# Two chained transformer layers on one core: the order of the work within a beat rebuilt on all engines

## The reference

```python
n = _layer_norm(x, ln1_g, ln1_b)
x = x + _attention(n, n, a1_wq, a1_wk, a1_wv, a1_wo, a1_bo)
n = _layer_norm(x, ln2_g, ln2_b)
x = x + _attention(n, context, a2_wq, a2_wk, a2_wv, a2_wo, a2_bo)
x = _geglu_ff(_layer_norm(x, ln3_g, ln3_b), ff_w1, ff_b1, ff_w2, ff_b2) + x
...
probs_t = jax.nn.softmax(scores_t, axis=-1)
text_out = jnp.einsum('bhst,bhtd->bhsd', probs_t, v_t)
qsem = _l2norm(jnp.einsum('bhst,bte->bhse', probs_t, text_ehs))
sem = jnp.einsum('bhse,bne->bhsn', qsem, _l2norm(ip_ehs))
probs_ip = jax.nn.softmax(attn_scores + SEM_SCALE * sem, axis=-1) * spatial_mask[None, None, :, None]
out = (text_out + ip_out) @ W_out + b_out + residual
```

## Time and profile before

| | us |
|---|---|
| median of 2 runs (4306.78 and 4325.45) | 4316.11 |
| the profiled execution | 4322.96 |
| its span, first to last instruction | 4321.2 |
| mean granted TensorE clock in it | 0.935 of full |

### The profile page before, as it was taken

The page is one execution under the profiler, slowest core; times in us unless marked ns, Lnnn a source line. Parts: engine busy times, 40 slices in busy tenths (PEclk is TensorE's granted clock), DMA queues, the critical chain, the costliest instruction groups (busy, mean ns, idle before and its releaser), DMA issues.

```text
span 4321.2 us, 96000 instructions
## 1 busy us (share of the span) xinstructions
PE 3645.5 (84%) x34752; PEld 3346.6 (77%) x34752; DVE 2540.2 (59%) x7677; ACT 2432.8 (56%) x6547; POOL 1337.3 (31%) x1657
## 2 busy tenths in 40 slices
PE   6889888888888988889788898888889888897887
PEld 5778778787777878878787787877778787787876
DVE  6546565565656656565565555656566565655654
ACT  4465555555555565565555655555555655655553
POOL 2223332333333323333233323333333233332322
PEclk8999999999999999999999989999999999999985
DMA  5422212222221312213122121322213222131210
GB/s 157 138 60 85 73 50 89 56 86 68 61 88 50 98 57 74 84 46 94 52 88 71 50 89 54 91 66 61 88 49 95 58 73 84 43 98 51 81 41 9
DMA packets 210732, 313.83 MB, mean 73 GB/s; under 512 B 31232, under 2 KB 167520, under 8 KB 210272
## 3 DMA queue, kind: packets, MB, share of 16 engines
q1 hardware_dynamic: 209984, 307.53, 24.3%
q10 hardware_dynamic: 288, 0.16, 0.0%
HBM read 267.97 MB, written 14.42 MB: 65 GB/s over the span
## 4 chain that ended last, share of the span: by engine, by line
PE 56%; DVE 22%; ACT 12%; issue 10%; POOL 0%; DMA 0%; SPq 0%; DVEq 0%; ACTq 0%; POOLq 0%
PE PG L623 7%; PE PW L755 5%; PE PV L809 5%; PE PS L775 5%; PE PG L598 4%; PE PV L858 4%; ACT SE L977 4%; PE PG L615 4%; PE PT L793 4%; DVE mx L1231 3%; PE PG L599 2%; PE PG L601 2%; PE PG L600 2%; PE PT L841 2%; PE PG L699 2%
## 5 line engine op out<-in xcount | busy, mean ns | idle before, releaser
L1433 POOL TENSOR_TENSOR SE<-SE,rs 128x512 f32<-128x512 f32 (+1 forms) x640 | 558.8, 873 | 2016.0 <-DVE rs L1253 2016.0
L977 ACT ACTIVATE SE<-PS,mx 128x77 f32<-128x77 f32 (+1 forms) x2560 | 677.6, 360 | 141.6 <-DVE mx L1231 140.2
L1426 POOL TENSOR_TENSOR n<-qq,p_half 128x4 f32<-128x4 f32 x320 | 323.4, 1010 | 688.8 <-DVE qq L1276 688.8
L965 ACT ACTIVATE PTs<-PT 128x1024 f32<-128x1024 f32 (+1 forms) x320 | 327.0, 1022 | 365.1 <-PE PT L793 365.1
L1169 DVE COPY v_sb<-PG 128x512 f32<-128x512 f32 (+1 forms) x320 | 220.5, 689 | 376.2 <-PE PG L623 219.3
L1248 DVE TENSOR_REDUCE sums<-SE 128x4 f32<-128x512 f32 (+1 forms) x640 | 365.7, 571 | 120.8 <-ACT SE L977 119.3
L995 ACT ACTIVATE SE<-PT,mx 128x73 f32<-128x73 f32 x1280 | 304.5, 325 | 208.8 <-DVE mx L1240 157.8
L755 PE MATMUL PW<-w_o,OTs 128*128 128x160 f32 x2560 | 404.8, 301 | 0.0
L913 ACT ACTIVATE qk<-PG 128x512 f32<-128x512 f32 (+1 forms) x640 | 328.6, 513 | 116.1 <-PE PG L601 109.7
L809 PE MATMUL PV<-PTs,v_sb 128*64 128x128 f32 (+1 forms) x5120 | 392.9, 301 | 0.0
L793 PE MATMUL PT<-ident,SE 64*128 64x64 f32 (+1 forms) x5120 | 255.8, 244 | 160.1 <-issue 155.0
(11 more groups left out here) (207 smaller groups left out, 8800.4 us busy)
## 6 DMA issues: line engine op xcount, KB each, us to landing
q_slice<-q_split SPq DMA_DIRECT2D x630, 192.0 KB, 2.4
vc_slice<-vc_split SPq DMA_DIRECT2D x155, 512.0 KB, 3.7
kc_slice<-kc_split SPq DMA_DIRECT2D x150, 256.0 KB, 2.7
q1st<-q_hi SPq DMA_DIRECT2D x320, 32.0 KB, 1.8
k1st<-k_hi SPq DMA_DIRECT2D x160, 38.5 KB, 2.2
xres<-in_x_dram SPq DMA_DIRECT2D x32, 160.0 KB, 2.4
q1st<-q_lo SPq DMA_DIRECT2D x160, 32.0 KB, 1.9
out_dram<-x SPq DMA_DIRECT2D x64, 80.0 KB, 1.9
```

The costliest lines, as they stand in the source:

```text
L965: a_(PTs[0:J, q % 2, :, :].rearrange("p u (i r k) -> p r (u i) k", r=2, k=64), PT[0:J, :, :].rearrange("p r (x k) -> p r x k", k=64), ACT. ...
L977: last = a_(SE[:, n % 4, J * i:J * i + J], PS[:, e, J * at:J * at + J], ACT.Exp, bias=mx[:, q % 2, 4 * e + at:4 * e + at + 1])
L1433: gp.tensor_tensor(e, e, rs[:, n % 2, :].unsqueeze(2).to_broadcast([128, 4, J]), ALU.mult)\
```

## The change

Nothing is computed otherwise. What moves:

- **PE**: layer 1's `probs_transposed1` and `scores1` come first in slot 1, ahead of the second `qk` job; `probs_v1` comes first in slot 2, ahead of `wo`.
- **ACT**: `exp1` moves from slot 0 of the next beat to slot 2 of its own beat; `pt1_out` moves ahead of the second `exp`.
- **DVE**: `softmax1_in` moves from slot 2 to slot 1, between the two `prob_sums`; the `v` read-out goes behind the second `prob_sums`; the sum of squares leaves `unit_out` and becomes `unit_norms`, right behind the maximum of slot 0 one beat later; the norm's pieces and the context's scaling go right behind it, `norm_out` three slots after `norm_stats`; `unit_out` goes ahead of `block_out`.
- **POOL**: `norms_of` one beat later, in slot 0; `rstd_of` and `add_bias` in the slot of the statistics.
- **Slots**: norms, `ff`, `down`, `q1`, context, x and tail jobs get other slots (most late jobs now stand in slot 2), `L1_BEAT` becomes `BEATS + 2`; the tail of an image is spread over 12 slots, not 8.
- **Buffers**: the gated tile `gl` moves from `shared` into rows 0 and 1 of `kx`, the cross-attention keys, free at that time; `csq` moves into row 9 of `kx`. The context's loads no longer wait for `ff`.

```diff
-    NORM_SLOT = {(0, 0): -16, (0, 1): -1, (1, 0): 17, (1, 1): 32, (2, 0): 47, (2, 1): 62, (3, 0): 56, (3, 1): 71}
-    FF_SLOT = [51, 52, 53, 53, 54, 66, 67, 68, 68, 69]
+    NORM_SLOT = {(0, 0): 42, (0, 1): 3, (1, 0): 18, (1, 1): 33, (2, 0): 48, (2, 1): 69, (3, 0): 60, (3, 1): 84}
+    NEXT_GROUP = {(0, 0)}
+    TURN_AFTER = [5, 5, 4, 1]
+    FF_SLOT = [53, 53, 53, 56, 56, 74, 74, 74, 77, 77]
...
-    PREP_SLOT = [14, 20]
-    X_SLOT = [11, 57]
-    L1_BEAT = BEATS + 1
+    PREP_SLOT = [-5, 13]
+    CONTEXT_SLOT = [-12, 0]
+    X_SLOT = [24, 60]
+    L1_BEAT = BEATS + 2
...
+    TAIL_JOB = {"ipT": 7, "ip": 9, "oT1": 10, "y": 12}
...
-        cin, gl = shared[0:TS, :, :], shared[:, :, :]
+        cin = shared[0:TS, :, :]
...
+        gl = kx[:, 0:2, 0:HT]
...
-            + [(t + (1 if k == 3 else 3), ("xT", g, k, h)) for t, g, k, h in NORMS]
+            + [(t + TURN_AFTER[k], ("xT", g, k, h)) for t, g, k, h in NORMS]
...
-            + [(STEP * g + PREP_SLOT[h] + 3, ("cT", g, h)) for g in range(GROUPS) for h in range(2)]
-            + [(tail_slot(g, b) + d, (kind, g, b)) for d, kind in ((5, "ipT"), (6, "ip"), (7, "oT1"), (8, "y"))
+            + [(STEP * g + PREP_SLOT[h] + 4, ("cT", g, h)) for g in range(GROUPS) for h in range(2)]
+            + [(tail_slot(g, b) + d, (kind, g, b)) for kind, d in TAIL_JOB.items()
...
+                    if part == 1 and l1_at(beat - 1):
+                        probs_transposed1(*l1_at(beat - 1), turned)
+                    if part == 1 and l1_at(beat):
+                        scores1(*l1_at(beat), turned)
                     for name in qk_at(t):
                         job(name)
                     for name in late_at(t):
                         if name[0] == "v":
                             job(name)
-                    if part == 1 and l1_at(beat - 1):
-                        probs_transposed1(*l1_at(beat - 1), turned)
-                    if part == 1 and l1_at(beat):
-                        scores1(*l1_at(beat), turned)
+                    if part == 2 and l1_at(beat - 1):
+                        probs_v1(*l1_at(beat - 1), multiplied)
...
-                    if sub == 0 and l1_at(beat - 1):
-                        exp1(*l1_at(beat - 1))
                     if sub == 0 and duo_at(beat):
                         pt_out(*duo_at(beat))
+                    if sub == 1 and l1_at(beat - 1):
+                        pt1_out(*l1_at(beat - 1))
...
-                    if sub == 1 and l1_at(beat - 1):
-                        pt1_out(*l1_at(beat - 1))
+                    if sub == 2 and l1_at(beat):
+                        exp1(*l1_at(beat))
...
+                    if sub == 0 and l1_at(beat - 2):
+                        unit_norms(*l1_at(beat - 2))
                     for g, h in preps_at(t - 2):
                         context_scale(g, h)
...
-                    for g, k, h in norms_at(t - 2):
+                    for g, k, h in norms_at(t - 3):
                         if k < 3:
                             norm_out(g, k, h)
```

More of the change, by code:

```diff
@@ L355, in norm_slot @@
             own = FIRST_NORM_SLOT if g == 0 else {}
-            return STEP * g + own.get((k, h), NORM_SLOT[(k, h)])
+            return STEP * (g - ((k, h) in NEXT_GROUP)) + own.get((k, h), NORM_SLOT[(k, h)])
         NORMS = sorted((norm_slot(g, k, h), g, k, h) for g in range(GROUPS) for k, h in NORM_SLOT)
@@ L885, in _ @@
                         wo(g, 2 * d + 1)
-                    if part == 2 and l1_at(beat - 1):
-                        probs_v1(*l1_at(beat - 1), multiplied)
                     for name in late_at(t):
@@ L1003, in context_squares @@
                         act.wait_ge(S["c_dve"], HB * (2 * g + h))
-                    if g > 0:
-                        for w in range(W1):
-                            act.wait_ge(S[f"k1_in{w}"], 16 * 3 * g)
                     for b in range(HB):
@@ L1458, in _ @@
                         normalise(g, 2 * d + 1)
[L1459 removed]
+                    for g, k, h in norms_at(t):
                         if k < 3:
@@ L1469, in _ @@
                         gp.tensor_tensor(cst[:, 1, :], cst[:, 0, :], p_half[0:TS, 0:HB], ALU.pow).then_inc(S["c_pow"], 1)
-                    if sub == 2 and l1_at(beat - 1):
-                        norms_of(*l1_at(beat - 1))
+                    if sub == 0 and l1_at(beat - 2):
+                        norms_of(*l1_at(beat - 2))
 _INS = ['x', 'ctx_2048', 'fside_S_0',
```

78 lines of the change are left out of this document (39 added, 39 removed).

## The result

The changed kernel takes 3682.97 us (median of 2 runs, 3681.71 to 3684.23) against 4316.11 before: ratio 0.853, 95% interval 0.845 to 0.861. The forecast was 4005 with a range of 3880 to 4190, so the sign was right and the gain, 633 us, was twice the 312 of the sum.

The account below looks back on a forecast made before the run. PE's work order and waits bound the kernel: 36.8 us idle a group less 14.0 and 5.0 leaves 17.8, plus 3.0 clock, times 15 is 312; edges 0. From 4322.96 to 4011, median 4005 us, range 3880 to 4190.

Parts of the forecast that it names:

- What goes: PE's listed waits in a full group, such as L793 (155.0 us) and `nx` (116.5): all 36.8 us of idle time removed.
- What comes: New PE waits the new order brings to each full group, four items from a walk through the engines' lists: 14.0 us.
- Late jobs of slot 1: Jobs right behind `v` wait for the second `qk` bank in six self-attention beats: 3.6 us a group.
- The Exp table's return: ACT's table load behind `pt_out` in four beats delays both `exp` and `qk` read-outs: 2.8 us a group.
- Bank chains: Slot 2 waits on PE: feed-forward piece behind context transposes 2.1, `k1` behind `xT` 1.35, `vip` 1.1; together 4.5 us.
- the allowance: Idle time put back on PE for waits the hand-made list missed: 0.25 us a beat, 5.0 a group.
- the clock: PE's busy time returned by a higher granted clock as idle time falls: 3 us a group, bounds 0 and 10.
- the edges: Group 0 and the tail behind the last scores: 5 us back on one, +5 on the other, together 0.
- Bound by PE alone: Rival: allowance not needed and clock returns with idle time, 440 us gained, 3877 us; 13%.
- The loop of DVE and ACT: Rival: this loop sets self-attention beats, adding 1.1 us a beat over ten beats, 11 a group: 4170 us; 18%.
- Slower, ACT the engine waited for: Rival: `exp1` comes later than PE's next L793, a wait in every beat costing 400 us: 4405 us; 4%.
- Norm pieces beside POOL: `norm_out` on DVE beside POOL's power op, 0 to 1.0 us added to each: taken as 0, 90 us if uncovered.

Follow-up runs that it names:

- a mere filler: Four dummy matmuls put ahead of PE's wait for `exp1` (before `probs_transposed`) in the kernel before: 4305.7 us, ratio 0.999.
- the parts put back: Changed kernel with one part put back at a time: `exp1` 3938.9 us, feed-forward pieces spread 3908.4, norm pieces ahead of the maximum 3876.8, layer 1's maximum in slot 2 3882.9.
- the two edits on listed waits: Changed kernel with `pt1_out` behind the second `qk` read-out: 3675.0 us; changed kernel with late jobs reordered (`k1`, `vip` ahead of `xT`, `cT` last): 3687.9.
- the first experiment: Kernel before with only layer 1's `exp1` moved to slot 2 of its own beat: 4303.8 us, ratio 0.997.
- the fastest version: Changed kernel with `pt1_out` behind the second `qk` read-out in 13 beats of 20: 3602.1 us; with `cT` also last in its slot 3601.1.

## Why the forecast was half the gain

*What goes* was right, row by row, for the waits themselves: L793 155.0 to 3.7, `nx` 116.5 to 16.5, no releaser of the earlier trace rows left among the large ones. It was not right as a set of separate amounts, though the sum did not need that: the 155.0 of L793 alone are worth 14 us (with 60 table loads more), and the whole set 633.

*What comes, 14.0 a group*: group 7 has 13.4, the mean is 13.0. By items:

1. Late jobs of slot 1, 3.6. PE waits 0.68, 0.68, 0.67, 0.87, 1.24 and 0.68 in the six beats: 4.8. Of the 1.24, 0.56 belong to the next item. Two rows of group 7:

```profile
1622.31 0.39 PE L608 MATMUL PG<-w_v_hi,nT 128*128 128x256 f32 x1 [0.34 <-ACT qk L915]
1624.76 0.54 PE L733 MATMUL PG<-vbd_sb,ipTs 80*128 80x160 f32 x2 [1.24 <-ACT qk L915]
```

2. The Exp table's return, 2.8. `v` waits 0.34 to 0.37 in three of the four beats, as in the first of these rows, and the late job behind it the 0.56: 1.6.
3. Bank chains, 4.5. They are 1.47, 1.55 and 0.88: 3.9. The first two in group 7:

```profile
1614.50 0.39 PE L600 MATMUL PG<-nT,w_hi 128*128 128x256 f32 x1 [1.47 <-DVE cipT L1150]
```

```profile
1720.63 1.17 PE L617 MATMUL PG<-cT,w_k1h 128*128 128x328 f32 x6 [1.55 <-DVE nT L1157]
```

4. Key beats, 3.1. `v` waits 0.28 in four beats and 0.45 in one, and smaller ones follow: 2.9. One that was not listed, 0.75 before `probs_v` behind the end of `unit_out`, makes the rest.

**The first step that failed is the allowance**, 5.0 us a group "since a list made by hand misses waits". The walk had missed one wait of 0.75; the kernel has 24.7 us less idle time a group, the list said 22.8, the sum took 17.8. Of these 6.9, 5.0 are the allowance, 0.9 that the mean group had 37.7 us of idle time and group 7 had 36.8, and 1.0 that less came than was listed. Over 15 groups this is 103 us.

**The second is the clock**, 3 us a group, where busy time fell by 14.4. Two errors lie in it. The forecast kept the light matmuls as a reason for the low clock; but they are as many as before, and the clock came back (26.6 to 4.2 us a group), as it did with a mere filler. And the forecast knew of no other way in which busy time could shrink; the upper bound of 10 was too low for that. A wait also makes the first matmuls behind it slow. Rows of the changed kernel, a `qk` job in flow and `v` behind a wait, both at the full clock:

```profile
1607.76 0.28 PE L600 MATMUL PG<-nT,q_slice 128*128 128x256 f32 x1
1607.88 0.28 PE L601 MATMUL PG<-nT,q_slice 128*128 128x256 f32 x1
...
1609.24 0.39 PE L608 MATMUL PG<-w_v_hi,nT 128*128 128x256 f32 x1 [0.36 <-ACT qk L915]
1609.46 0.28 PE L609 MATMUL PG<-w_v_lo,nT 128*128 128x256 f32 x1
```

In flow the starts are 0.12 apart; behind the wait the first takes 0.22 to the second, 0.39 to its end, and the pipeline's end before it (0.28 behind the last start) counts as busy while nothing new begins. In the stretch of the earlier trace rows at the lower clock the same jobs start 0.21 apart. Over the 16 kernels of this study without fillers, the means per group (1 to 14) lie on a line: busy time = 204.5 + 0.51 x idle time, correlation 0.97; from 13.0 us idle and 209.4 busy (changed) over 19.5 and 215.7 (norms before the maximum) to 37.7 and 223.9 (before). How the 0.51 divides between clock and restarts the runs tell only roughly, since the two go together: with both in the fit a microsecond at the lower clock adds 0.36 of busy time and one of idle time 0.22. From 26.6 to 4.2 that is 8 us for the clock and from 37.7 to 13.0 5.4 for the restarts, near the 14.4.

The groups of one kernel part the two better, since they hold the same instructions in the same order and still differ in their clock. Two groups of the kernel before (PE's columns alone):

```profile
1285.96:1545.27 259.31, 219.07 (x2175) 0.97 0.25 72
2330.82:2600.11 269.29, 234.68 (x2175) 0.90 0.24 69
```

With the clock not rounded, the low-clock time is 13.7 and 51.2 us. Over groups 2 to 14 a microsecond of it adds 0.41 us of busy time in the kernel before (r = 1.00) and takes 0.15 of idle time away, so the group is 0.26 longer; in the changed kernel it adds 0.47 and idle time stays at 13.2 to 13.4. Without any low-clock time the lines end at 213.4 and 208.5 us of busy time. So of the 14.4 us some 9.5 are the clock and some 4.9 are there at the full clock too. Restarts would account for these: a group of before has 43 waits above 0.05 us on average, a changed one 24, and each costs by the rows above about 0.26 us of busy time (0.10 in the first start and 0.16 of the pipeline's end), so the 19 fewer are worth 4.9 us, an estimate. The same two groups have one order of instructions and two clocks, so the order alone does not set the clock. Nor does the amount of idle time alone: layer 1's chain alone in the kernel before took 7.6 us of idle time from a group, and its low-clock time did not fall.

Over 15 groups the step is short by 171 us.

**The third is the edges**, taken as nothing: 60 us. Group 0 lost 21 us of idle time and 11 of busy time. It has the same norm and context transposes as every group, whose waits I had counted for full groups only: in group 0's window of before PE waits 10.2 us for `nx` and 4.8 for `shared`, and the beats with them were 3 to 6 us longer than they are now. The tail lost 28 us, which went back when `exp1` was put back and partly (12 us) with layer 1's maximum: the steps of layer 1 there have nothing of layer 0 beside them, so the lateness of the chain stood in each. `exp1` alone in the kernel before took 2 us off the tail, the chain 12. It takes 6.2 us a step now (143.68 over 23) in place of 7.8. I had used the 7.8 for the step added and did not ask why it was 7.8.

103 + 171 + 60 is 334, where the forecast was 327 above the profiled execution (4011 against 3684). The 7 too many are group 15, counted here as a full group: it gained 32 us where the mean of the others is 39.

The rivals. *Bound by PE alone* (3877, 13%) was the right one in kind and still too small, by the clock's step and the edges. *The loop of DVE and ACT* did not add its 1.1 us a beat. That the engines' lists do bind is seen from the parts put back, which cost about 200 us each. That the two edits on listed waits gained only 8 and -5 us speaks less for it, since the first of them gained 81 once it was placed by beat. How long this loop is, no run measured. *Slower, ACT the engine waited for* did not come; it was the state of the first experiment, where `exp1` moved without its maximum and with 60 table loads more, and even there the time was the same. *Table loads*: 129, as forecast (127 to 129), but not worth nothing wherever they stand: spread between two `exp`, 182 more loads and the new slots of their jobs cost 225 us. An `exp` still starts right behind its load (1607.56 behind one that ends at 1607.54 in group 7, which itself starts 0.02 behind `pt_out`), so the drain that the Trainium skill (ScalarE: Activation LUTs, section What ACT_TABLE_LOAD costs) adds is not seen in this kernel either.

*Norm pieces beside POOL*, taken as 0 with 90 us if uncovered: the collision is there, and POOL pays. In one norm of the changed kernel DVE's four `nx` pieces keep their 0.34 and POOL's power op takes 1.57 where it took 1.01:

```profile
1735.98 0.34 DVE L1112 SCALAR_TENSOR_TENSOR nx<-lt,rstd,ln_b 128x128 f32<-128x128 f32 x1
1736.14 1.57 POOL L1433 TENSOR_TENSOR n<-qq,p_half 128x4 f32<-128x4 f32 x1 [5.88 <-DVE qq L1281]
1736.24 0.34 DVE L1114 SCALAR_TENSOR_TENSOR nx<-lt,rstd,ln_b 128x128 f32<-128x128 f32 x1
```

The power op's mean rose from 1010 to 1118 ns, and the `nx` piece fell from a mean of 573 to 343, in group 7 its longest from 1129 to 348: it now meets the power op, no more the multiplication. By the rule of the Trainium skill (SBUF — State Buffer, section Who interferes with whom) the two exclude each other; the trace agrees that they collide. In the kernel before DVE's piece was the long one, here it is POOL's op, which had slack. The one that starts second pays: POOL's multiplication began at 1845.63, ahead of the long piece of the earlier trace rows at 1845.72, and here DVE's first piece began at 1735.98, ahead of POOL's op at 1736.14. It holds for all in both traces: each of the 125 pieces of before that took over 0.4 us met an op of POOL that had begun first, and each of the 59 long power ops of the changed kernel (over 1.15 us) met a piece that had begun first.

## What to carry to other kernels

Where several engines hand a beat round, the largest row of waits is not the gain of removing it: judge the whole order at once, and expect a part alone to bring little until the loops beside it are as short. Count the table loads of every order, also of one that is only an experiment: one instruction moved here added 60. If the walk through all lists finds that PE's idle time falls, take busy time along with it (here half a microsecond for each of idle time) and put the same account to the first and last stages. An edit that helps in most beats and hurts in some is to be placed by beat, from the measured length of each.

## What the runs showed of the hardware

PE can do useless work in a wait at no loss: 1192 fillers, 260 us from their starts to the next real matmul, left the time at 0.999 of before, and the granted clock of group 7 rose from 0.94 to 0.96. In the changed kernel with `exp1` put back, filled and unfilled took the same 3939 us with 0.978 and 0.956 of the clock. What the clock gives back is not all time: between groups of the kernel before a microsecond at the lower clock made the group 0.26 us longer, in the changed kernel, where PE waits less, 0.45. Where DVE's two-input piece and an op of POOL overlapped, the one that had started second was the long one, in 125 and 59 cases. What stays open is what sets the low-clock time of a group, which differs from 13.7 to 51.2 us between groups of one kernel, and which wait ends the beats of the fastest version.
